# Splitting the shift values on GpSimd, one wait fewer before the exponentials, and another order of items and products

## What is computed

```python
x = x + 0.5 * ffn(layernorm(x))          # ffn: [x,-x] -> 1024 -> 1024 -> 256, weights +1/-1
x = x + attn(layernorm(x))               # 16 heads of width 16, causal, softmax over 2048 keys
x = x + 0.5 * ffn(layernorm(x))

scores = einsum('bhqd,bhkd->bhqk', q, k) / sqrt(16)
scores = where(causal, -1e9, scores)
ctx = einsum('bhqk,bhkd->bhqd', softmax(scores), v)
return ctx @ w_o.T + b_o
```

## Time and profile before

| | |
|---|---|
| median of 3 runs | 1597.89 us (1595.64 to 1599.81) |
| the profiled execution | 1595.7 us, its span 1593.6 us |
| granted TensorE clock | 0.998 |
| PE busy | 1562.7 us (98%) |
| DVE busy | 1146.8 us (72%) |
| ACT busy | 846.3 us (53%) |
| POOL busy | 157.5 us (10%) |

### The profile page before, as it was taken

One profiled execution on the slowest core, in us unless ns is written; L12 is line 12 of the kernel. 1 busy time (PEld: TensorE's weight loads), 2 busy tenths in 40 slices (PEclk: granted clock), 3 DMA queues, 4 the chain that ended last, 5 costly groups with the idle time before them and its releaser, 6 DMA issues.

```text
span 1593.6 us, 36067 instructions
## 1 busy us (share of the span) xinstructions
PE 1562.7 (98%) x14224; PEld 729.0 (46%) x14224; DVE 1146.8 (72%) x1758; ACT 846.3 (53%) x1702; POOL 157.5 (10%) x320
## 2 busy tenths in 40 slices
PE   7999999999989999999999999999999999999998
PEld 3555555555433333333333333333333555555554
DVE  6535543554569999999999999999996666666552
ACT  3222322322148888888887888888886222222221
POOL 4300000000011011111111111111111000000000
PEclk9999999999999999999999999999999999999999
DMA  5011013101041222212222211222212111100400
GB/s 182 1 53 53 5 48 92 53 0 53 1 121 46 69 68 62 64 40 41 68 68 62 68 39 47 60 68 62 68 62 86 54 53 53 47 23 35 132 13 14
DMA packets 115763, 89.05 MB, mean 56 GB/s; under 512 B 76080, under 2 KB 95152, under 8 KB 115632
## 3 DMA queue, kind: packets, MB, share of 16 engines
q1 hardware_dynamic: 115632, 87.20, 19.1%
HBM read 49.15 MB, written 37.75 MB: 55 GB/s over the span
## 4 chain that ended last, share of the span: by engine, by line
PE 97%; DVE 1%; ACT 1%; issue 1%; DMA 0%; DVEq 0%
PE ffn_mm L426 28%; PE ffn_mm L1226 18%; PE ffn_mm L1246 15%; PE ffn_mm L412 7%; PE ffn_acc L442 7%; PE ffn_acc L598 6%; PE ffn_tr L598 5%; PE ffn_mm L697 3%; PE ffn_acc L709 2%; PE ffn_acc L518 2%; PE ffn_tr L399 1%; PE ffn_tr L603 1%; PE ffn_acc L603 1%; DVE m_part L618 1%; ACT probs L1198 1%
## 5 line engine op out<-in xcount | busy, mean ns | idle before, releaser
L1198 ACT ACTIVATE probs<-ffn_mm 128x512 f32<-128x512 f32 (+3 forms) x1280 | 605.2, 544 | 137.7 <-PE ffn_mm L1226 128.7
L618 DVE TENSOR_REDUCE m_part<-ffn_acc 128x2 f32<-128x1024 f32 (+2 forms) x345 | 367.9, 1066 | 45.8 <-PE ffn_acc L598 34.8
L426 PE MATMUL ffn_mm<-ffn_h1h,w 128*128 128x512 f16 x1024 | 388.2, 379 | 0.0
L426 PE MATMUL ffn_mm<-ffn_h1l,w 128*128 128x512 f16 x1024 | 388.1, 379 | 0.0
L1226 PE MATMUL ffn_mm<-qk 66*32 66x512 f16 (+7 forms) x5120 | 382.6, 354 | 1.9 <-ACT probs L1198 1.3
L618 DVE TENSOR_REDUCE m_part<-ffn_tr 128x2 f32<-128x1024 f32 (+3 forms) x295 | 310.5, 1053 | 20.7 <-PE ffn_tr L603 11.2
L1246 PE MATMUL ffn_mm<-probs,v 128*32 128x512 f32 (+3 forms) x2560 | 303.2, 532 | 0.2
L472 ACT ACTIVATE ffn_h2h<-ffn_mm 128x512 f16<-128x512 f32 x128 | 76.4, 597 | 303.7 <-PE ffn_mm L426 302.5
L483 DVE SCALAR_TENSOR_TENSOR ffn_h2l<-ffn_mm,ffn_h2h 128x512 f16<-128x512 f32 x128 | 85.7, 686 | 185.0 <-ACT ffn_h2h L472 185.0
L1226 PEld LDWEIGHTS ffn_mm<-qk 66*32 66x32 f16 (+1 forms) x5120 | 120.9, 94 | 210.6 <-ACT probs L1198 102.2
L1161 POOL TENSOR_SCALAR_AFFINE_SELECT probs<-probs 128x256 f32<-128x256 f32 (+1 forms) x256 | 107.2, 425 | 676.3 <-ACT probs L1198 672.3
(11 more groups left out here) (112 smaller groups left out, 1136.7 us busy)
## 6 DMA issues: line engine op xcount, KB each, us to landing
qk<-qk_scr SPq DMA_DIRECT2D x256, 64.0 KB, 2.7
ctx_scr<-ctx_out SPq DMA_DIRECT2D x64, 256.0 KB, 2.5
qk<-ctx_scr SPq DMA_DIRECT2D x64, 256.0 KB
v_scr<-v_pad SPq DMA_DIRECT2D x32, 256.0 KB, 2.9
v<-v_scr SPq DMA_DIRECT2D x16, 512.0 KB, 4.5
x_res<-L_attn_x SPq DMA_DIRECT2D x8, 512.0 KB, 3.5
qk_scr<-qk_hi SPq DMA_DIRECT2D x32, 128.0 KB, 1.8
qk_scr<-qk_lo SPq DMA_DIRECT2D x32, 128.0 KB, 1.8
```

Source lines behind the costliest of these rows:

```text
L426: ins = nc.tensor.matmul(f.mm[:, m % 4, :], w1[:, kt, m * P:(m + 1) * P], part[:, kt, :], start=(kt == 0 and part is f.h1h), stop=(kt == H ...
L618: nc.vector.tensor_reduce(m_part[u][:, t, :, r], s_ps[slot][:, :, 0:w], AX.X, ALU.max).then_inc(sb.s_done, 1)
L1198: nc.scalar.activation(probs[:, g % P_SLOTS, j, c0:CH], st_ps[bank(k)][:, c0:CH], ACT.Exp, scale=scale_now).then_inc(se.exp_done, 1)
```

## The change

It has four parts.

1. The two split operations leave DVE. A new function `pool_columns` does them on GpSimd in three operations: `m_low` = scaled `m_neg` in float32, `m_col[..., 0]` = its float16 copy, `m_col[..., 1]` = the difference. DVE keeps `m_neg`, with a new wait for the previous chunk's `m_cols`.
2. GpSimd's program takes the calls in: two before the last `add_bias` of phase A, one ahead of the masks, and the others between the masks, at the place that `ITEM_POINTS` gives to the chunk's last unit.
3. ACT loses its wait for the products of four steps before, at the first exponential of a step.
4. `PV_POINTS` and `ITEM_POINTS` have other values. `TURN_DELAY`, the sequence of the items and all tile shapes are as they were.

```diff
-PV_POINTS = (1, 1, 2, 1, 2, 1, 3, 2, 3, 2, 2, 0, 1, 0, 1, 0, 2, 2, 3, 1)
+PV_POINTS = (2, 2, 2, 3, 0, 0, 1, 3, 3, 3, 3, 1, 2, 0, 1, 0, 2, 2, 2, 0)
-ITEM_POINTS = (5, 5, 14, 20, 22, 24, 24, 28, 32, 37, 41, 48, 49, 55, 55, 61, 67, 73, 73, 76, 77, 78, 78, 85,
-              89, 94, 95, 102, 102, 107, 111, 118, 119, 126, 129, 129, 138, 138, 143, 145, 145, 152, 152, 159)
+ITEM_POINTS = (8, 8, 18, 21, 24, 27, 27, 32, 36, 38, 46, 47, 52, 56, 60, 63, 66, 70, 77, 77, 79, 81, 81, 90,
+              91, 97, 97, 102, 103, 107, 111, 118, 119, 125, 128, 128, 138, 138, 142, 146, 147, 151, 159, 159)
...
                 if units.index(x) == last_unit[i]:
                     wait(nc.vector, sb.s_done, use + 1)
+                    wait(nc.vector, sb.m_cols, chunks)
                     nc.vector.tensor_reduce(m_neg.rearrange("p h t -> p t h"), m_part[u][:, i * TPC:(i + 1) * TPC, :, 0:i + 1], AX.X,
                                             ALU.max, negate=True).then_inc(sb.m_neg, 1)
-                    wait(nc.vector, sb.m_neg, chunks + 1)
-                    nc.vector.tensor_scalar(m_col[:, :, 0, :], m_neg[:, :, :], 1.0 / M_SCALE, None,
-                                            ALU.mult).then_inc(sb.m_hi, 1)
-                    wait(nc.vector, sb.m_hi, chunks + 1)
-                    nc.vector.scalar_tensor_tensor(out=m_col[:, :, 1, :], in0=m_neg[:, :, :], scalar=1.0 / M_SCALE,
-                                                   in1=m_col[:, :, 0, :], op0=ALU.mult, op1=ALU.subtract).then_inc(sb.m_cols, 1)
...
+        def pool_columns(chunks):
+
+            wait(nc.gpsimd, sb.m_neg, chunks + 1)
+            nc.gpsimd.sem_inc(sb.gate_pool, 1)
+            nc.gpsimd.tensor_scalar(m_low[:, :, :], m_neg[:, :, :], 1.0 / M_SCALE, 0.0, ALU.mult, ALU.add).then_inc(sb.m_low, 1)
+            wait(nc.gpsimd, sb.m_low, chunks + 1)
+            nc.gpsimd.tensor_copy(m_col[:, :, 0, :], m_low[:, :, :]).then_inc(sb.m_hi, 1)
+            wait(nc.gpsimd, sb.m_hi, chunks + 1)
+            nc.gpsimd.tensor_tensor(m_col[:, :, 1, :], m_low[:, :, :], m_col[:, :, 0, :], ALU.subtract).then_inc(sb.m_cols, 1)
...
                 for g in range(ALL_STEPS):
+                    pair, s = divmod(g, STEPS)
+                    for j in range(4):
+                        if diagonal(s) and j % 2 == 1:
+                            mask(g, j // 2)
+                        for _, owner, x, use in items(pair, s, j):
+                            if x in ends_chunk:
+                                pool_columns(owner * QCH + x[1] // TPC)
...
-                        if j == 0:
-                            wait(act, se.pv_done, g - P_SLOTS + 1)
                         wait(act, se.st_ready, k + 1)
```

More of the change, by code:

```diff
@@ L176, in __init__ @@
         self.m_neg = new("m_neg")
+        self.m_low = new("m_low")
         self.m_hi = new("m_hi")
@@ L292, in build @@
         m_neg = sbuf(top, "m_neg", [P, 2, TPC], F32)
+        m_low = sbuf(top, "m_low", [P, 2, TPC], F32)
         m_col = sbuf(top, "m_col", [P, 2, 2, TPC], F16)
@@ L832, in _, with add_bias @@
                 pool.wait_ge(se.bo_in, 16)
-                with pool.Fori(0, NCH) as c:
+                def add_bias(c):
                     pool.wait_ge(ln2.sem.xn, c + 1)
@@ L837, in _ @@
                         nc.gpsimd.tensor_tensor(x_tile(c, t), x_tile(c, t), bo_row[:, :], ALU.add).then_inc(sb.bo_add, 1)
+                with pool.Fori(0, NCH - 1) as c:
+                    add_bias(c)
+                for i in range(2):
+                    pool_columns(i)
+                add_bias(NCH - 1)
             @block.vector
@@ L1149, in _, with mask @@
             def _(pool):
-                for g in range(ALL_STEPS):
[L1151 to L1163, removed]
+                def mask(g, par):
+                    s = g % STEPS
+                    i = chunk_of[s]
+                    kb, _, c0 = step_slots(s)[2 * par]
+                    w = (kb - TPC * i + 1) * P - c0
+                    pool.wait_ge(se.exp_done, 4 * g + 2 * par + 2)
+                    pool.sem_inc(se.gate_pool, 1)
+                    view = probs[:, g % P_SLOTS, 2 * par:2 * par + 2, c0:c0 + w]
+                    nc.gpsimd.affine_select(out=view, in_=view, compare_op=ALU.is_ge, fill=0.0,
+                                            base=c0 - (kb - TPC * i) * P, pattern=[[0, 2], [1, w]],
+                                            channel_multiplier=-1).then_inc(se.mask_done, 1)
+                ends_chunk = [units[n] for n in last_unit.values()]
+                for x in AHEAD[len(EARLY):]:
+                    if x in ends_chunk:
+                        pool_columns(x[1] // TPC)
+                for g in range(ALL_STEPS):
+                    pair, s = divmod(g, STEPS)
[3 more added lines that the diff above has]
+                        for _, owner, x, use in items(pair, s, j):
+                            if x in ends_chunk:
+                                pool_columns(owner * QCH + x[1] // TPC)
             @block.vector
```

## The result

| | before | after |
|---|---|---|
| median | 1597.89 us (1595.64 to 1599.81, 5 runs) | 1588.86 us (1587.79 to 1590.09, 5 runs) |
| the profiled execution | 1595.7 us, span 1593.6 us | 1588.9 us, span 1587.1 us |
| its granted TensorE clock | 0.998 | 0.996 |

The ratio is 0.9941, with a 95% interval of 0.9927 to 0.9954: faster by 9.0 us, where 16 us were forecast against the median. The time lies inside the range, 7 us above the forecast.

A forecast was written before the change was run, and what follows sets the result against it. PE bounds the kernel, waiting about 1.9 us of each 47.35 us attention pair. Pairs of 46.4 us save 0.95 each, 14.3 us over fifteen, plus 0.5 in the last: 1582 us forecast, range 1570 to 1591.

The forecast's parts named there:

- waiting for VectorE: PE's stalls for DVE's reductions in an attention pair: 1.5 us before, 0.4 us left by the more even order.
- 28 runs instead of 27: The new order breaks a pair's units into one more consecutive group, costing PE 0.2 us a pair.
- 45.5 + 0.2 + 0.4 + 0.35: New attention pair: PE's work, one more run of units, waiting left for DVE, waiting for banks; 46.4 us.
- The purse: All the time PE really waits in an attention pair, the most that could be gained: about 1.9 us.
- 20 items start when DVE lets go: Of a pair's 44 items, 20 start within 0.2 us of the end of the reduction two before; excess 1.5 us.
- the banks (0.35, taken as unchanged): Score groups in a pair wait for a PSUM bank that ACT still reads: 0.35 us, the same after the change.
- the 1.9: DVE's time saved per attention pair by moving the split to GpSimd: 1.9 us, from 43.4 to about 41.6.
- ACT's wait: 0: Dropping the exponentials' wait for earlier products in attention gains nothing; bounds 0 and 0.3 us a pair.
- GpSimd's chain: Three small split operations on GpSimd plus semaphore pickup, per chunk: 1.05 us, between 0.9 and 2.4 us.
- the cover: Time from the end of `m_neg` to T0 that hides GpSimd's split: 1.68 us; beyond it PE waits one for one.
- Hidden, but barely: Next pair's q and k loads between T2 and U0.0: 13.3 to 13.6 us left, 13.4 needed; cost taken as 0.
- a rival at 0.13 for 5 to 9 us: Next pair's loads stall PE at U0.0, 0.3 to 0.6 us a pair, giving 1586 to 1591 us; chance 0.13.

The follow-up runs named there:

- the kernel without late loads and with T2 in its place: U0.0 moved four points later in ITEM_POINTS against the changed kernel, T2 left: 1588.97 us, on a chip where the kernel before had 1598.68.
- the second trace of the changed kernel: The changed kernel run once more, nothing altered, beside the kernel before on the same chip: 1587.77 us beside 1598.57, ratio 0.9931.

## Why the prediction was right, and where it was not

| per quiet pair, us | forecast | measured |
|---|---|---|
| waiting for VectorE | 1.5 to 0.4 | 0.9-1.2 to 0.2-0.3 |
| waiting for banks | 0.35, unchanged | about 0.7 to 0.36 |
| 28 runs instead of 27 | +0.2 | +0.2 (0.215 a run) |
| sum | -0.95 (46.4) | -0.88 (46.47) |
| jitter, 14 pairs together | 0 | +3.0 |

**The sign, the mechanism and the pair held.** 46.47 us is what "45.5 + 0.2 + 0.4 + 0.35" came to within 0.1. 15 pairs x 0.88 = 13.2 us, and 0.6 for the last pair (forecast 0.5): 13.8. Less 3.0 of jitter, 10.8 are left, and 10.6 are measured at equal clock. The forecast's sum was 14.8.

**The purse was divided wrongly, and two errors cancelled.** "20 items start when DVE lets go" was true (21), but the excess of 1.5 us that I put down to them was not all DVE's: halve the reductions and 0.93 us go, and with the waits still seen then it is about 1.2. I counted an item's whole excess as a wait for DVE if it started just behind a reduction. The step failed there. On the other side "the banks (0.35, taken as unchanged)" was half of what they were, and they did not stay: the new order and the dropped wait took 0.36 us from them. -1.1 and 0 were forecast, -0.7 to -0.9 and about -0.36 came. The purse itself was about right: 0.9 to 1.2 and 0.7 are 1.6 to 1.9 us. And DVE's busy time fell by 1.4 us a pair to 42.0, not by 1.9 to 41.6: the 1.9 were distances from start to start, not busy times.

**"ACT's wait: 0" was wrong** within its bounds of 0 to 0.3: 0.12 alone, 0.15 with the rest. I argued from ACT's idle time: the wait ends none of it. But it lies between two exponentials of a full stretch, where ACT isn't idle, and presumably each costs a little of ACT's pace just where TensorE waits for a bank (2.13 against 2.07 us for four exponentials).

**GpSimd's chain was right**: 1.05 against 0.94 us, 0.6 against 0.63 us between columns and T0, and the price beyond the cover one for one. Only the cover was put too high, 1.68 us instead of 1.43. By the estimate from the Trainium skill ("GPSIMD Engine Reference", sections 3 and 8, twice VectorE's time) each of the three would have taken 0.34 us; they took 0.20, 0.19 and 0.20 where DVE's took 0.17, so for operations this small the rule is far too high here.

**The loads were the failed step that cost the most.** "Hidden, but barely: cost 0 to 0.3 us a pair, I take 0", with a rival at 0.13 for 5 to 9 us. The middle of the range was right: the loads take 12.3 to 14.3 us from T2 to the last landing, and the order gives 13.5. What was missing is that they vary. One number of a quiet place was compared with another, when the question was how often the one passes the other: in 5 of 14 pairs, 1.4 us in all. The spread was there to be read in the trace of the kernel before: in its 14 pairs the last landing comes 12.7 to 13.7 us after T2, and the new order leaves 13.2 us for it (13.5 less the 0.3 from landing to U0.0). So the rival was not false either, only at most a third of its size: the kernel without late loads and with T2 in its place was no faster.

**The other 1.6 us of jitter were in no rival.** 0.15 us come at the same items of the same pairs in kernel after kernel (the eleventh item of the second pair, for one, in all seven traces of the new order with full reductions), and a few waits of 0.4 to 1.3 us come and go.

**The base**: "that one lies at the low end of the three runs, which would make 1583" saw the difference and gave it 1 us where it was 2 to 3. With 1598.6 as the base and the sum of 14.8 the forecast would have been 1584; the change gave 1588.

## What to carry to other kernels

A stall is whose it is by what goes away when that engine's work is taken away, not by whose end it follows; make that kernel, it is a change of one line, and look at which waits are left in it. Where the margin of a transfer is within the spread of its own durations, price it by how often it is late, and look at all its occurrences in the trace, not at one. And before two profiled executions are compared, compare their clocks: here 3 of 10.6 us lay in that.

## What was not expected of the hardware

- Issuing a q or k load takes 0.42 us, but in nearly every pair one of the sixteen, in the new order several times two, takes 0.5 to 2.1 us. With T2 a point earlier it is mostly one. I don't know what holds them.
- Some waits of TensorE end with nothing that the program does. In the second trace of the changed kernel T3 of the fourteenth pair came 1.3 us late (TensorE idle for 1.14 of them), though the chain's columns were ready at 1096.14:

```profile
1096.43 1.03 PE L1267 MATMUL ffn_mm<-probs,v 128*32 128x512 f32 x8
1098.60 0.22 PE L609 MATMUL ffn_tr<-ident_h,m_col 128*16 128x128 f16 x1 [1.14 <-issue]
```

In the DMA view of the 2.9 us before it one packet is of another kind than the data's:

```profile
q1 hardware_dynamic: 148, 0.26, 25.1%
q8 instruction: 1, 0.02, 2.8%
```

It is a load of instructions, begun at 1095.82 us. Of the seven waits over 0.35 us at such places that I followed in four traces, six end 2.6 to 3.1 us after a packet of this kind began, the seventh 4.6 us. Such packets are common, though, 109 in the attention phase of this trace, one in 7 us, and nearly all pass without a wait. That TensorE waited for its instructions there is argued from this, not shown: no run took the packets away, and what these waits are stays open.
